# Attention scores from two 12-bit pieces in the one-pass 32-bit type, with the maxima added by TensorE

## What is computed

```python
# A: 16 heads; q, k, v of 2 x 8 numbers per head, rotary tables on q and k
q1, q2 = jnp.split(q * cos + rotate_half(q) * sin, 2, axis=-1)      # k alike
attn1 = einsum('bhid,bhjd->bhij', q1, k1) * scale                    # 128 x 128, depth 8
attn2 = einsum('bhid,bhjd->bhij', q2, k2) * scale
probs = softmax(attn1) - lam * softmax(attn2)
out = einsum('bhij,bhjd->bhid', probs, v) @ W_proj                   # v: 16 numbers per head
# D: 16 heads of 8 numbers, causal
attn = softmax(where(causal, q @ k^T, -inf) / sqrt(8)); y = attn @ v @ Wout + bout
```

## Time and profile before

| | |
|---|---|
| median of three runs | 631.55 us (631.34 to 631.91) |
| the profiled execution | 630.57 us, span 628.8 us |
| first attention, scores to last output (A) | 35.1 to 171.2 us |
| causal attention (D) | 278.3 to 354.0 us |
| busy share | PE 88%, DVE 43%, ACT 36%, POOL 13% |

### The profile page before, as it was taken

The page is one execution under the profiler, slowest core; times in us unless marked ns, Lnnn a source line. Parts: engine busy times, 40 slices in busy tenths (PEclk is TensorE's granted clock), DMA queues, the critical chain, the costliest instruction groups (busy, mean ns, idle before and its releaser), DMA issues.

```text
span 628.8 us, 12335 instructions
## 1 busy us (share of the span) xinstructions
PE 553.6 (88%) x4854; PEld 401.8 (64%) x4854; DVE 272.6 (43%) x679; ACT 223.5 (36%) x406; POOL 84.0 (13%) x131
## 2 busy tenths in 40 slices
PE   8658999999886899828999859999999899999994
PEld 3446777777664389415566636677777667677764
DVE  4333444442147643503243359666672325223325
ACT  1202433433323142000245426665665062443340
POOL 4000111111131000200000044322222100000001
PEclk9755555555588699955599979999999998999998
DMA  7522221200303000122110000000100000111110
GB/s 224 199 102 100 89 71 69 74 33 2 134 1 134 1 2 2 40 96 100 68 39 24 34 11 10 13 11 11 44 1 1 1 25 23 46 34 34 35 41 33
DMA packets 22637, 31.66 MB, mean 50 GB/s; under 512 B 5428, under 2 KB 13956, under 8 KB 22336
## 3 DMA queue, kind: packets, MB, share of 16 engines
q1 hardware_dynamic: 22592, 31.01, 14.7%
HBM read 26.68 MB, written 4.12 MB: 49 GB/s over the span
## 4 chain that ended last, share of the span: by engine, by line
PE 76%; DVE 12%; DMA 6%; ACT 3%; issue 1%; POOL 1%; SPq 0%; POOLq 0%; DVEq 0%; ACTq 0%
PE ps L563 16%; PE ps L942 9%; PE ps L925 9%; PE ps L585 7%; PE ps L841 4%; PE ps L558 4%; PE ps L598 3%; PE ps L814 2%; PE ps L913 2%; DMA near<-stacks 2%; DMA stacks<-arena 2%; PE ps L822 2%; PE ps L830 2%; PE ps L749 2%; PE ps L783 2%; PE ps L864 2%
## 5 line engine op out<-in xcount | busy, mean ns | idle before, releaser
L1241 DVE TENSOR_REDUCE negm<-ps 128x4 f32<-128x512 f32 x96 | 61.9, 686 | 124.1 <-PE ps L563 124.1
L990 ACT ACTIVATE probs<-ps 128x512 f32<-128x512 f32 (+1 forms) x100 | 56.5, 590 | 97.6 <-PE ps L563 97.2
L563 PE MATMUL ps<-near 8*128 8x128 f32 (+1 forms) x768 | 76.7, 420 | 13.0 <-DMA near<-stacks 6.9
L563 PEld LDWEIGHTS ps<-near 8*128 8x128 f32 (+1 forms) x768 | 65.9, 309 | 28.5 <-issue 22.8
L563 PE MATMUL ps<-w1a 8*128 8x128 f32 (+1 forms) x768 | 69.4, 385 | 0.0
L942 PEld LDWEIGHTS ps<-w1a,arena 128*128 128x128 f32 x512 | 61.0, 196 | 7.2 <-issue 6.2
L990 ACT ACTIVATE arena<-ps,w1a 128x512 f32<-128x512 f32 x64 | 43.4, 687 | 60.6 <-PE ps L925 59.4
L563 PEld LDWEIGHTS ps<-w1a 8*128 8x128 f32 (+1 forms) x768 | 59.2, 277 | 8.4 <-issue 8.4
L1550 DVE SCALAR_TENSOR_TENSOR racc<-ps,sm,racc 128x128 f32<-128x128 f32 x128 | 36.0, 344 | 64.7 <-PE ps L942 64.6
L942 PE MATMUL ps<-w1a,arena 128*128 128x128 f32 x512 | 61.4, 280 | 0.8 <-DVE racc L1541 0.8
L925 PE MATMUL ps<-xT,w1a 128*128 128x512 f32 x128 | 57.9, 594 | 1.4 <-ACT xT L990 1.4
(11 more groups left out here) (180 smaller groups left out, 725.3 us busy)
## 6 DMA issues: line engine op xcount, KB each, us to landing
near<-stacks SPq DMA_DIRECT2D x24, 256.0 KB
w1a<-stacks SPq DMA_DIRECT2D x24, 256.0 KB
stacks<-arena SPq DMA_DIRECT2D x6, 512.0 KB
w1a<-in_w1a SPq DMA_DIRECT2D x1, 2048.0 KB, 7.7
w2a<-in_w2a SPq DMA_DIRECT2D x1, 2048.0 KB, 7.8
w1a<-in_w1b SPq DMA_DIRECT2D x16, 128.0 KB, 2.0
w1a<-in_w2b SPq DMA_DIRECT2D x16, 128.0 KB, 2.1
con<-in_con SPq DMA_DIRECT2D x1, 644.0 KB, 5.7
```

The source lines that it names most:

```text
L563: last = mm(o[:, cols], left[rows, cols], right[rows, cols], start=not causal, stop=not causal or k == 3)
L990: return nc.scalar.activation(o, i, f, **kw)
L1241: nc.vector.tensor_reduce(negm[:, n % 2, 4 * g:4 * g + 4], tiles(bank(RING_S[(4 * n + g) % 3]), 4, P), AX.X, ALU.max, negate=True).then_in ...
```

## The change

It is in both attentions. A query or key q is split in q_hi (its upper 12 significant bits, by a mask on the integer view) and q_lo = q - q_hi. The 32 rows of a quadrant now hold, for each of the 8 numbers, the four pairs hi and lo of the queries with hi and lo of the keys, and the matmul is of type float32r, the 32-bit type with one pass. The two pieces are written to `stacks` separately and repeated on loading, by a dimension with step 0. Each slot takes three loads instead of two: 64 rows outermost for the keys, 32 for each piece of the queries.

A step is rearranged: it is now four heads of one half with four batches, so that in A the first eight steps are the heads' first halves and the last eight the second ones (`place`). `outputs` of the first halves go straight to `oall`; only the second halves pass through POOL's `add_outputs`.

The maxima are not moved by a DMA. DVE writes their upper 12 bits four times to `mparts`, POOL the rest, PE transposes all 128 columns, ACT copies them to `mT` (128 rows, float32r), and each transposed score gets one more matmul, whose weights `pick` (a table of zeros and ones) choose the two rows that belong to it.

In the entry of A the pieces are made by DVE (high ones, low keys) and POOL (low queries), in a new order; SP loads the first slots as soon as the first half's pieces are written. In D the same follows the projections. Two calls of `keep_busy` grow: from 6 to 8 matmuls ahead of A, from 18 to 30 ahead of D.

```diff
-LOADS = 2
+PIECES = 2
+HEAD_BITS = -4096
+LOADS = 3
+        def place(v, count):
+            return v // (count // 2), v % (count // 2) // 2, v % 2
...
-                    sp.dma_start(tile, bass.AP(stacks, (t * NH + h) * HEAD, [[HALF, 4], [ROW, QUAD], [1, HALF]])
-                                 ).then_inc(a.stack[h % FLIGHT], 16)
+                sp.dma_start(keys_of[slot].bitcast(F32), bass.AP(stacks, KEYS + 4 * HD * m * ROW + at, [[ROW, 8 * HD], [0, 2], [1, HALF]])
+                             ).then_inc(signal, 16)
+                for p in range(PIECES):
+                    sp.dma_start(queries_of[slot][p:P:2, :].bitcast(F32), bass.AP(stacks, p * P * ROW + at, [[ROW, 4 * HD], [0, 2], [1, HALF]])
+                                 ).then_inc(signal, 16)
-            def move_maxima(a, n, slot):
-                sp.wait_ge(a.mc, n + 1)
-                sp.dma_start(queries_of[slot][MROW:MROW + 3 * QUAD + 1:QUAD, :], mT[:, n % 2, :]
-                             ).then_inc(a.mrow[n % FLIGHT], 16)
...
+            sp.wait_ge(A.hi, 1)
+            keep_keys(0, 0)
+            sp.wait_ge(A.hi, 2)
+            keep_queries(0, 0)
+            sp.wait_ge(A.klo, 1)
+            keep_keys(0, 1)
+            sp.wait_ge(A.qlo, 1)
+            keep_queries(0, 1)
+            sp.wait_ge(A.kept, 16 * 4)
+            heads(A, 0, 4, NH)
...
+            def split_maxima(a, v):
+                pool.wait_ge(a.mhi, v + 1)
+                nc.gpsimd.tensor_tensor(mparts[:, v % 2, :, 16:32], over(negm[:, v % 2, :], 4), mparts[:, v % 2, :, 0:16],
+                                        ALU.subtract).then_inc(a.msplit, 1)
...
                 for k in range(4):
                     cols = slice(k * P, (k + 1) * P)
-                    for o, left, right, g, depth, _, done in cells:
-                        rows = slice(QUAD * g, QUAD * g + depth)
-                        last = mm(o[:, cols], left[rows, cols], right[rows, cols], start=not causal, stop=not causal or k == 3)
-                        if k == 3:
+                    for o, left, right, g, shift, _, done in cells:
+                        rows = slice(QUAD * g, QUAD * g + QUAD)
+                        last = mm(o[:, cols], left[rows, cols], right[rows, cols], start=not causal,
+                                  stop=shift is None and (not causal or k == 3))
+                        if k == 3 and shift is None:
                             last.then_inc(done, 1)
+                    for o, left, right, g, shift, _, done in cells:
+                        if shift is not None:
+                            rows = slice(QUAD * g, QUAD * g + QUAD)
+                            last = mm(o[:, cols], pick[rows, k, :], shift[rows, :], start=False, stop=not causal or k == 3)
+                            if k == 3:
+                                last.then_inc(done, 1)
...
-                        pe.wait_ge(a.mrow[n % FLIGHT], (a.turns + n // FLIGHT + 1) * 16)
+                        pe.wait_ge(a.mc, n + 1)
...
-            keep_busy(6, BANK_M0)
+            keep_busy(8, BANK_M0)
...
-            keep_busy(18, BANK_M0)
+            keep_busy(30, BANK_M0)
...
+                def high_maxima(n):
+                    dve.wait_ge(a.max, 4 * n + 4)
+                    if n >= 2:
+                        dve.wait_ge(a.mt, n - 1)
+                    ts(mparts[:, n % 2, :, 0:16].bitcast(I32), over(negm[:, n % 2, :], 4).bitcast(I32), HEAD_BITS, None,
+                       ALU.bitwise_and).then_inc(a.mhi, 1)
...
+            def high_piece(a, n):
+                return ts(rope[:, 2 * n + 1, :].bitcast(I32), rope[:, 2 * n, :].bitcast(I32), HEAD_BITS, None, ALU.bitwise_and
+                          ).then_inc(a.hi, 1)
+            def low_keys(a, n, turn):
+                dve.wait_ge(a.hi, turn)
+                tt(rope[:, 2 * n, :], rope[:, 2 * n, :], rope[:, 2 * n + 1, :], ALU.subtract).then_inc(a.klo, 1)
```

More of the change, by code:

```diff
@@ L18 @@
 BF16 = mybir.dt.bfloat16
+F32R = mybir.dt.float32r
+I32 = mybir.dt.int32
 ALU = mybir.AluOpType
@@ L128, in decoder_kernel @@
         rw0 = sb("rw0", [P, E0])
+        with nc.sbuf_tensor("late", [P, 2, 4, HALF], F32R) as late:
+            pass
         w1a = sb("w1a", [P, E0, F0 * P])
@@ L336, in heads @@
[L336 to L357, removed]
+            def load_stacks(a, v, count):
+                c, m, half = place(v, count)
+                at = 4 * HD * m * ROW + (2 * c + half) * HALF
+                slot, signal = v % RING, a.stack[v % RING]
+                sp.dma_start(keys_of[slot].bitcast(F32), bass.AP(stacks, KEYS + 4 * HD * m * ROW + at, [[ROW, 8 * HD], [0, 2], [1, HALF]])
[3 more added lines that the diff above has]
+                                 ).then_inc(signal, 16)
@@ new lines, in heads, with keep_queries, keep_keys @@
+            def heads(a, first, count, total):
+                for v in range(first, first + count):
+                    if v >= RING:
+                        sp.wait_ge(a.st, 4 * (v - RING + 1))
+                    load_stacks(a, v, total)
+            def keep_queries(c, p):
+                sp.dma_start(bass.AP(stacks, p * P * ROW + c * T, [[ROW, P], [1, T]]), rope[:, 2 * c + 1 - p, :]).then_inc(A.kept, 16)
+            def keep_keys(c, p):
+                sp.dma_start(bass.AP(stacks, KEYS + p * ROW + c * T, [[2 * ROW, P], [1, T]]), rope[:, 4 + 2 * c + 1 - p, :]
+                             ).then_inc(A.kept, 16)
@@ L359, in _ @@
+            keep_queries(1, 1)
+            sp.wait_ge(A.qlo, 3)
+            keep_keys(1, 1)
+            sp.wait_ge(A.kept, 16 * 8)
+            heads(A, RING, RING, NH)
             sp.wait_ge(A.st, 4 * NH)
@@ L363, in _ @@
             load(w2a[:], d["w2a"], ld_f)
[L364 to L369, removed]
+            for p, (queries, keys) in enumerate(((D.hi, D.hi), (D.qlo, D.klo))):
+                sp.wait_ge(queries, 1)
+                sp.dma_start(bass.AP(stacks, p * P * ROW, [[T, P], [1, T]]), rope[:, 1 - p, :]).then_inc(D.kept, 16)
+                sp.wait_ge(keys, 2 - p)
+                sp.dma_start(bass.AP(stacks, KEYS + p * ROW, [[2 * ROW, PAIRS * HD], [T, 2], [1, T]]), rope[:, 3 - p, :]
+                             ).then_inc(D.kept, 16)
+            sp.wait_ge(D.kept, 16 * 4)
+            heads(D, 0, PAIRS, PAIRS)
             def weights(pair, slot):
@@ L426, in _ @@
             pch = Chain(pool, pchain)
[L428 to L445, removed]
-                pch.wait()
[L447 to L454, removed]
-                            pool.wait_ge(a.pv, n - 1)
[L456 to L471, removed]
@@ new lines, in heads @@
+            def heads(a, count):
+                pool.wait_ge(a.vall, 4 if a is A else 2)
+                split_maxima(a, 0)
+                split_maxima(a, 1)
+                for n in range(count + 2):
+                    if n < count:
+                        if n >= 2:
+                            pool.wait_ge(a.pv, n - 1)
+                        values(a, n, count)
+                    if n + 2 < count:
+                        split_maxima(a, n + 2)
+                    if a is A and n - 2 >= NH // 2:
+                        add_outputs(n - 2)
```

197 lines of the change are left out of this document (127 added, 70 removed).

## The result

The kernel after takes 609.2 us (median of four, 608.57 to 609.95), the kernel before on the same chip 631.55. The ratio is 0.9646, 95% interval 0.9627 to 0.9665: faster by 22.4 us, where 70.6 were forecast. It lies within the range and near the price of rival 3, 614.

What follows compares the result with a forecast made beforehand. PE at half clock was taken to bound A (first attention), PE also D (causal one), DMA their entries. A's 38.5, the clock's 13.6 and D's 18.7 sum to 70.8 off 630.6: 559.8, 561 on the median's scale; range 543 to 616.

Steps and rivals of the forecast that it cites:

- rival 3: Float32r streams two beats per column, so transposed score blocks gain nothing; 17.6 us saved, 614; chance 0.17.
- The score blocks: Blocks with transposed scores, at one beat per column: 1.17 us at low clock, 0.67 at high; 0.85 and 0.43 saved.
- The term of -26.1: A's 32 blocks with transposed scores at the low clock: 27.2 us saved, less 1.1 for the wider transpose of maxima.
- The upright blocks: Five blocks without transposed scores per entry: in A 1.6 us instead of 2.95 each; in D -6.4 together.
- The clock: Fuller rows raise TensorE's clock for part of A: half of 27 us, -13.6; chance 0.36.
- D's body: Sixteen halves with transposed scores in D: three at the low clock (-2.6), thirteen at the high one (-5.6).
- Entries and loads: Loads spread over 16 DMA engines and no moved row of maxima: A's entry -12.4 us, D's -4.1.
- Rivals 1, 2, 4, 5: A's clock low (575, 0.20) or high (547, 0.10); four beats (692, 0.11 with other losses); maxima as wait (573, 0.06).
- Clock low through A: TensorE stays at the low clock through all of A, at one beat per column: 575; chance 0.20.
- Four beats per column: Float32r streams at four beats, at the low clock: slower, 692; chance 0.11 together with other causes of loss.
- The split of maxima: DVE, POOL, PE and ACT in a row become a new wait each step: price 12 us, 573; chance 0.06.
- The rest: Rearranged values, outputs and additions only for second halves: same or fewer elements on engines with slack; nothing.

Runs made afterwards that it cites:

- probe: The kernel after with nine short series of unused matmuls of various types and widths appended at its end, at the high clock; one execution of 614.57 us.
- bf16_pick: The kernel after with the table that picks the maxima and the transposed maxima in bf16, scores still float32r; 595.32 us.
- kick_five: The kernel after with one bf16 filler matmul of 512 columns ahead of each bank of scores in A's first five steps with transposed scores; 574.07 us.
- f32_type: The kernel after with all four tiles of the scores in plain fp32 instead of float32r; 619.51 us.
- no_pick: The kernel after without the matmuls that add the maxima to the transposed scores; 543.87 and 544.67 us, in two further executions 555.57 and 556.35.
- load4c: The kernel after with loads whose outermost dimension is a repetition of 4 that can't be merged, so the scores are of other rows; 622.51 us.
- kick_before: The kernel before with bf16 filler matmuls ahead of the banks of scores in A's first five steps with transposed scores; 629.29 us.

## Why the prediction was right or wrong

**The score blocks: wrong, and the step that failed.** I took one beat per column from the bf16 row for a whole matmul, weight load and stream together. The probe shows one beat for the moving columns and two for the weights' (114 ns against 63 for bf16 at 128 by 128), and at this shape the load is the longer. Eight loads in the transposed groups make 8 x 0.213 us at the low clock: 1.90 us instead of 1.17, as long as the eight fp32 records of before. The block at the high clock is 1.05 to 1.11, not 0.67. The term of -26.1 measured -2.1. Per matmul the new type does cost half of fp32 (one load of 0.213 us instead of two records), not the quarter I took; the additions of maxima doubled the number of matmuls in the transposed groups and used that half up.

The Trainium skill (TensorE: Matmul & The Clock Gate, LDWEIGHTS) puts a weight load at 107 ns per 128 columns whatever the rows. That agrees with the new type at the high clock (114 ns from start to start), not with it at the low one (0.21 us), nor with bf16 (63 ns). I had set the rule aside because bf16 contradicted it; the row nearest in bytes, the fp32 weight load of 192 ns against bf16's 98, was the better witness, and I had it as rival 3.

**Rival 3: right in size, wrong in mechanism.** Its 614 is near 609.2, in part by luck: of its 17.6 us D was to give 8.4 and gave 5.9, and 2.0 us came from parts that it left alone. But it let the moving columns stream at two beats; they don't, and that matters for what to do: fewer weight columns or narrower weights help (bf16_pick), moving operands of up to 256 columns cost hardly more than 64 (122 ns against 110).

**The upright blocks.** Forecast 0.75 us at the low clock; 1.11 in the entry of A (36.86), 1.09 in D. Same cause: four loads are 4 x 0.213. A's first three blocks stood at the high clock with 0.63, 0.71 and 0.66 us, which by luck made A's entry come out right all the same, and D's upright blocks gave 4.8 instead of 6.4.

**The clock: wrong both ways.** I took half of 27 us, for fuller rows. The kernel after got none of it: A stayed at 0.50. Yet the high clock was worth more than I thought, also than the whole 27: 35 us between the kernel after and kick_five, since with PE's step at 7.28 it has more to halve. Fuller rows with fp32 (f32_type) and without the additions (no_pick) brought it up; the mix of this change did not. Why this mix stays low is open: the runs show which mixes rise, not the rule.

**D's body.** -8.2 forecast, +1.6 measured. The half step at the high clock is 3.1 us as before, by the same load bound. The clock stayed low for 21 us after the first transposed scores (276.0 to 297.0) instead of 16 (297.6 to 313.5), which at half clock is some 2.5 us (an estimate from these times); no run tells whether the change or chance delayed the rise.

**Entries and loads: right in mechanism, partly by luck in size.** The write and the loads at 302 GB/s, no moved row, A's entry -12.0 of -12.4, D's -2.7 of -4.1. In A a high piece took 0.65 to 0.69 us, not 1.25, and POOL's low queries 3.26 us, not 2.34; the two errors cancel, and the last write of the first half went out at 22.49 us for the 22.4 of the forecast. In D the last high and low pieces took 1.76 and 1.24 us ahead of the write; in A one high piece took 2.7 us with POOL at work beside it, behind the issue of the first load, where it cost nothing. load4c shows that the spread is about half of the whole gain.

**Rivals 1, 2, 4, 5.** Clock low through A is what happened, but with blocks of 1.90 us; in the kernel after only filler brought the high clock. Four beats per column fell with the probe. The split of maxima is no wait in the kernel after: at the low clock PE's chain runs from block to values to transpose without one. At the high clock, in no_pick, it did stand in the chain. **The rest**: 2.0 us after D and before the end, in blocks that the change doesn't touch; no run separates it.

## What to carry to other kernels

At 128 by 128 a one-pass 32-bit matmul took half of an fp32 one (upright block in D 1.09 us against 2.06), not a quarter, since the weight load, at two beats per column, sets its pace; a rewrite that doubles the number of matmuls loses that half again. So measure load and stream apart before pricing a type. By the probe the load is hidden only where the moving operand is wider than twice the weights. What cancels, such as a softmax shift, needs no 32-bit operands (bf16_pick, 595.32 us). When a stage bound by TensorE runs at half clock, try a few filler matmuls at its head (574.07 us with filler alone, 562.25 with bf16 additions, against 609.2), check over several executions that the clock does come up, and check that it stays, which it did not in the kernel before.

## What the hardware did that I had not expected

- The one-pass 32-bit type costs the same with 64, 128 and 256 moving columns: 110, 114 and 122 ns per matmul with 128 weight columns.
- Less work gave a higher clock: without the additions A's clock rose by itself, with them it was 0.50 over 84.0 us of which PE was busy all.
- Short pauses of PE do not tell whether the clock holds: with 0.67 us idle of 20 it stayed at 1.00 in no_pick, and in kick_before, with one pause of 0.4 us, it fell.
- A type that keeps PE longer did so too: fp32 in the same layout rose to 1.00 at about 69 us.
- The same integer mask over 128 x 1024 took DVE 0.65 to 0.69 us in four of six cases, and 1.76 and 2.71 in the two in which POOL's subtraction over as many numbers (L466) ran beside it for 1.2 and 2.2 us. No run separates the two engines. Two of the masks, with POOL's work between:

```profile
22.44 0.68 DVE L1346 TENSOR_SCALAR arena<-arena 128x1024 int32<-128x1024 int32 x1
...
25.29 2.35 POOL L466 TENSOR_TENSOR arena<-arena 128x1024 f32<-128x1024 f32 x1
...
25.48 2.71 DVE L1346 TENSOR_SCALAR arena<-arena 128x1024 int32<-128x1024 int32 x1
```
